# Second attention: keys and eight query heads projected first, the rest between the scores, the bias as a matmul

## The reference, cut to what matters

```
qkv = x @ Wqkv + bqkv            # 256 -> 384 columns: 32 query heads, 8 key heads, 8 value heads, 8 wide each
k, v = repeat(k, 4), repeat(v, 4)
scores = q @ k^T / sqrt(8)       # 512 tokens against 512, two batches, 32 heads
out = softmax(scores) @ v
out @ Wo + bo
```

## Time and profile before

| | |
|---|---|
| median of 3 runs | 675.0 us (671.65 to 675.63) |
| the profiled execution | 669.68 us, span of the trace 667.8 us |
| granted TensorE clock, mean | 0.986 |
| PE busy | 617.4 us, 92% of the span |
| DVE / ACT / POOL busy | 404.4 / 325.1 / 213.2 us |
| start of the attention's projections | 352.73 us from the span's start |
| first score matmul of the loop | 362.19 us |

### The profile page before, as it was taken

One profiled execution on the slowest core, in us unless ns is written; L12 is line 12 of the kernel. 1 busy time (PEld: TensorE's weight loads), 2 busy tenths in 40 slices (PEclk: granted clock), 3 DMA queues, 4 the chain that ended last, 5 costly groups with the idle time before them and its releaser, 6 DMA issues.

```text
span 667.8 us, 11795 instructions
## 1 busy us (share of the span) xinstructions
PE 617.4 (92%) x4298; PEld 408.0 (61%) x4298; DVE 404.4 (61%) x929; ACT 325.1 (49%) x645; POOL 213.2 (32%) x312
## 2 busy tenths in 40 slices
PE   3999999999999988799978999999999999989990
PEld 2887887887888785366665544444444445546660
DVE  4526705632760587533366999989998954743336
ACT  4523423433332224133215589898988875523322
POOL 5870561282073154513333031201010100331331
PEclk9999999999999999899989999999999999999996
DMA  6000200300199992222379994000000000031213
GB/s 220 33 1 33 96 1 20 107 1 1 38 283 299 78 314 77 78 58 81 105 237 346 303 180 3 1 1 2 2 1 2 1 2 1 9 104 55 81 56 126
DMA packets 69000, 57.40 MB, mean 86 GB/s; under 512 B 21520, under 2 KB 64400, under 8 KB 68944
## 3 DMA queue, kind: packets, MB, share of 16 engines
q1 hardware_dynamic: 66736, 50.60, 31.2%
q0 software_dynamic: 2208, 6.05, 2.5%
HBM read 30.78 MB, written 25.85 MB: 85 GB/s over the span
## 4 chain that ended last, share of the span: by engine, by line
PE 73%; DVE 16%; DMA 3%; ACT 3%; issue 2%; POOL 1%; SPq 1%; ACTq 0%; POOLq 0%; DVEq 0%
PE psum L303 9%; PE psum L305 8%; PE psum L304 8%; PE psum L1289 8%; PE psum L1634 8%; DVE mx L1744 7%; PE psum L1606 5%; PE psum L1318 5%; PE psum L1594 5%; PE psum L1619 3%; PE psum L1213 2%; DVE stat L666 2%; PE psum L1564 2%; PE psum L1282 2%; PE psum L1199 1%
## 5 line engine op out<-in xcount | busy, mean ns | idle before, releaser
L1744 DVE TENSOR_REDUCE mx<-psum 128x1 f32<-128x512 f32 x256 | 157.6, 681 | 17.6 <-PE psum L1606 17.5
L1505 ACT ACTIVATE pr<-psum 128x512 f32<-128x512 f32 x256 | 138.0, 598 | 27.9 <-PE psum L1619 26.1
L1634 PE MATMUL psum<-pr,vals 128*32 128x256 f32 x1024 | 77.6, 389 | 0.0
L1619 PE MATMUL psum<-qT,kT 32*128 32x512 f32 x256 | 76.6, 494 | 0.7 <-ACT pr L1505 0.7
L1606 PE MATMUL psum<-kT,qT 32*128 32x512 f32 x256 | 67.7, 488 | 1.7 <-ACT qT L1472 0.7
L1289 PE MATMUL psum<-w_gu,xgT 128*128 x120 | 56.4, 592 | 0.0
L624 POOL DMA_INDIRECT routed_y<-yr,xg x30 | 28.7, 958 | 86.1 <-DVE yr L876 85.5
L1606 PEld LDWEIGHTS psum<-kT,qT 32*128 32x128 f32 x256 | 26.3, 181 | 43.9 <-issue 21.4
L1546 POOL CAST mp<-mx 128x16 bf16<-128x16 f32 x16 | 3.1, 196 | 150.5 <-DVE mx L1744 150.5
L867 DVE SCALAR_TENSOR_TENSOR h<-psum,xg,sg 128x256 f32<-128x256 f32 x30 | 14.5, 484 | 49.8 <-ACT sg L1046 49.8
L1046 ACT ACTIVATE sg<-psum,xg 128x256 f32<-128x256 f32 x30 | 14.2, 474 | 60.4 <-PE psum L1289 60.4
(11 more groups left out here) (214 smaller groups left out, 1406.6 us busy)
## 6 DMA issues: line engine op xcount, KB each, us to landing
sorted_x<-zeros SPq DMA_DIRECT2D x2, 9088.0 KB, 39.2
w_gu<-in_L_ffn_gate_w SPq DMA_DIRECT2D x16, 256.0 KB, 6.2
w_gu<-in_L_ffn_up_w SPq DMA_DIRECT2D x16, 256.0 KB, 6.3
w_d<-in_L_ffn_down_w SPq DMA_DIRECT2D x16, 256.0 KB, 6.6
xg<-sorted_x SPq DMA_DIRECT2D x30, 129.0 KB, 2.2
wk_f<-in_L_attn_Wk SPq DMA_DIRECT2D x4, 512.0 KB, 5.2
wq_f<-in_L_attn_Wq SPq DMA_DIRECT2D x4, 512.0 KB, 6.0
wv_f<-in_L_attn_Wv SPq DMA_DIRECT2D x4, 512.0 KB, 3.7
```

The costliest lines, as they stand in the source:

```text
L1505: nc.scalar.activation(pr[d % 3][:, j], s2_bank(d, j), ACT.Exp, scale=SCALE).then_inc(exp_ready, 1)
L1619: mm(s2_bank(d, j), kT[n // GH][rows, kc * P:(kc + 1) * P], qT2[n % 2][rows, :], start=True, stop=True).then_inc(s2_made, 1)
L1634: last = mm(ps[AV_BANK][j * VW:(j + 1) * VW, cols], vals[:, n // NKV * TB + kc, n % NKV // GH * GH + j, :], pr[d % 3][:, j, cols], start=( ...
L1744: v.tensor_reduce(mx[n % 2][:, t, j:j + 1], s1_bank(c, j), AX.X, ALU.max, negate=True).then_inc(max_read, 1)
```

## The change

- The first four tiles: PE projects only 128 columns at first (the first eight query heads, two groups, and all keys) with `project_first`. ACT rounds the high parts straight from PSUM (`first_hi`), DVE subtracts the low parts of keys and queries straight from PSUM (`first_low`), and this now stands between DVE's statistics of the second half of x. The keys and first queries are turned when the new semaphore `first_stacked` has reached 4.
- The other 256 columns of these tiles (24 query heads and the values) are projected by `project_rest` in two accumulations of 192 and 64 columns: tile 0 ahead of the loop, tiles 1 and 2 in the steps c = 0 and 1, tile 3 at the end of step c = 2. ACT takes each (`take_rest`); POOL rounds and subtracts.
- The bias is a third matmul in each accumulation: a row of ones against the bias row (`with_bias`).
- The second batch's takes (c = 3 to 6) go from DVE to ACT, without the addition. `complete(1)` is cut in three pieces behind the takes of the steps 3, 4 and 5 (2, 3 and 3 tiles).
- The second half of x is turned into banks 6 and 7 in place of 4 and 6, and a turn of queries waits until ACT has copied these.
- Of the ten groups of `keep_warm`, the counts and places change: four and one matmuls ahead of the loop, two in each of the steps 0 and 1.

```diff
-        TURN_X = ((4, 5, 6, 7), (0, 1, 0, 1), (0, 1, 4, 6), (0, 1, 0, 1))
+        TURN_X = ((4, 5, 6, 7), (0, 1, 0, 1), (0, 1, 6, 7), (0, 1, 0, 1))
...
-            close_x(1, 1)
-            l1_y = dve_l1(dve, link, mark, settle, y_tiles, close_stats, sum_x)
+            sum_x(1, 1)
+            l1_y = dve_l1(dve, link, mark, settle, y_tiles, close_stats, sum_x, stats_x)
...
-            def hi_parts(b, t):
-
-                act.wait_ge(qkv_ready, b * TB + t + 1)
-                stack_hi(nc.scalar, b, t, "k").then_inc(k_hi_made[b], 1)
-                stack_hi(nc.scalar, b, t, "q").then_inc(q_hi_made[b], 1)
+            def first_hi(t):
+
+                first = ps[QKV_BANK[t]]
+                act.wait_ge(qkv_made, t + 1)
+                stack_hi(nc.scalar, 0, t, "k", (0, NKV), first[:, FQ:2 * FQ]).then_inc(k_hi_made[0], 1)
+                stack_hi(nc.scalar, 0, t, "q", (0, FH), first[:, 0:FQ]).then_inc(q_hi_made[0], 1)
+
+            def take_rest(t):
+                act.wait_ge(rest_made, t + 1)
+                nc.scalar.activation(qkv[:, t, FQ:FQ + HALF], ps[REST_BANK[t]][:, 0:HALF], ACT.Copy).then_inc(qkv_ready, 1)
+
+            def take(t):
+                act.wait_ge(qkv_made, t + 1)
+                nc.scalar.activation(qkv[:, t, :], ps[QKV_BANK[t]][:, 0:QKV], ACT.Copy).then_inc(qkv_ready, 1)
...
             for what in FIRST:
                 copy_turn(what)
+            take_rest(0)
             normalise(2, 1)
+            take_rest(1)
             for c in range(END):
                 d = c - LAG
+                if c == 1:
+                    take_rest(2)
                 if c == 2:
                     turn_copy(2, 2)
                     turn_copy(2, 3)
-                    complete(1)
+                if c == QKV_AT:
+                    take_rest(3)
+                if QKV_AT <= c < min(QKV_AT + TB, LAG):
+                    take(TB + c - QKV_AT)
+                    if c + 1 < QKV_AT + TB:
+                        complete(1, range(NT)[(c - QKV_AT) * NT // 3:(c + 1 - QKV_AT) * NT // 3])
...
+                if LAG <= c < QKV_AT + TB:
+                    take(TB + c - QKV_AT)
...
+            def with_bias(o, t, cols):
+
+                for c in range(KC):
+                    mm(o, xT[:, c, t * P:(t + 1) * P], cols(wqkv[:, c]), start=(c == 0), stop=False)
+                return mm(o, ones[0:1, :], cols(bqkv[0:1, :]), start=False, stop=True)
+
+            def project_first(t):
+
+                pe.wait_ge(xT_ready, 4 * 2 + t // 2 + 1)
+                with_bias(ps[QKV_BANK[t]][:, 0:2 * FQ], t,
+                          lambda w: w.rearrange("p (a n) -> p a n", a=2)[:, :, 0:FQ]).then_inc(qkv_made, 1)
+
+            def project_rest(t):
+
+                if t >= 2:
+                    pe.wait_ge(qkv_ready, t - 1)
+                with_bias(ps[REST_BANK[t]][:, 0:HALF - FQ], t, lambda w: w[:, FQ:HALF])
+                with_bias(ps[REST_BANK[t]][:, HALF - FQ:HALF], t, lambda w: w[:, KEND:QKV]).then_inc(rest_made, 1)
...
                 elif n >= 2:
                     wait_read(pe, TURNS[n - 1])
+                    pe.wait_ge(xT_ready, 4 * 2 + 4)
                 else:
-                    pe.wait_ge(qkv_ready, TB)
+                    pe.wait_ge(first_stacked, TB)
...
             for t in range(TB):
-                project_qkv(t)
-            pe.wait_ge(qkv_ready, TB)
-            keep_warm(3, 3)
+                project_first(t)
+            keep_warm(4, 3)
             turn(FIRST[0])
-            keep_warm(4, 3)
+            keep_warm(1, 3)
             turn(FIRST[1])
+            project_rest(0)
             for c in range(END):
...
-                if c < QKV_AT:
-                    keep_warm(2, 3)
+                if c < 2:
+                    project_rest(c + 1)
...
-                if c < QKV_AT:
-                    keep_warm(2, 3)
+                if c < 2:
+                    keep_warm(2, AV_BANK)
+                if c == 2:
+                    project_rest(3)
...
+            def first_low(t):
+
+                first = ps[QKV_BANK[t]]
                 dve.wait_ge(k_hi_made[0], t + 1)
-                stack_lo(v, 0, t, "k").then_inc(k_stacked[0], 1)
-
-            for t in range(TB):
-                take(t)
-                if t:
-                    key_lo(t - 1)
-            key_lo(TB - 1)
+                dve.wait_ge(q_hi_made[0], t + 1)
+                stack_lo(v, 0, t, "k", (0, NKV), first[:, FQ:2 * FQ]).then_inc(k_stacked[0], 1)
+                stack_lo(v, 0, t, "q", (0, FH), first[:, 0:FQ]).then_inc(first_stacked, 1)
+
+            stats_x(1, first_low)
...
-                if QKV_AT <= c < QKV_AT + TB:
-                    take(TB + c - QKV_AT)
```

More of the change, by code:

```diff
@@ L77 @@
 SCALE = float(1.0 / HD ** 0.5)
+HALF = NQ * HD
+FH = 2 * GH
+FQ = FH * HD
 def build(nc, a, out):
@@ L212, in build @@
         vals = at("vals", [P, NT, NKV, VW], F32, l1)
-        bqkv, bqkv_in = (at(n, [P, QKV], F32, l1) for n in ("bqkv", "bqkv_in"))
+        bqkv, bqkv_in = (at(n, [P, w], F32, l1) for n, w in (("bqkv", 2 * HALF), ("bqkv_in", QKV)))
         wqkv_in = at("wqkv_in", [P, KC, QKV], F32, l1)
-        wqkv = at("wqkv", [P, KC, QKV], F32, l1)
+        wqkv = at("wqkv", [P, KC, 2 * HALF], F32, l1)
         wo1 = at("wo1", [P, KC, D], F32, l1)
@@ L283, in build @@
         qkv_made, qkv_ready, turn_copied = (sem(n) for n in ("qkv_made", "qkv_ready", "turn_copied"))
+        rest_made, first_stacked, rest_hi = (sem(n) for n in ("rest_made", "first_stacked", "rest_hi"))
         k_hi_made, q_hi_made, k_stacked, q_stacked = (per_layer(n) for n in ("k_hi_made", "q_hi_made", "k_stacked", "q_stacked"))
@@ L700, in sum_x, with stats_x @@
                         mark(ins)
-            def stats_x(half):
+            def stats_x(half, between=None):
                 for i in range(TB):
@@ L706, in stats_x @@
                     tile_stats(x, half * TB + i)
+                    if between:
+                        between(i)
                 close_stats(0, half)
@@ L980, in normalise, with complete @@
                                          scale=rstd[0][:, t:t + 1]).then_inc(xn_ready[half], 1)
-            def complete(p):
-                for t in range(NT):
+            def complete(p, tiles=range(NT)):
+                for t in tiles:
                     if p == BLOCKS - 1:
@@ L1449, in places, with stack_hi @@
             return tile[b][:, t].rearrange("p h (n d) -> p h n d", d=HD)[:, :, first:first + (n - 1) * step + 1:step, :]
[L1451 to L1455, removed]
+        def stack_hi(eng, b, t, kind, heads=None, src=None):
+            tile, n, at_, first = (qs, NQ, Q_AT, 0) if kind == "q" else (ks, NKV, K_AT, HALF)
+            from_, to = heads or (0, n)
+            if src is None:
+                src = qkv[:, b * TB + t, first + from_ * HD:first + to * HD]
+            dst = places(tile, b, t, at_)[:, from_:to].bitcast(F32R)
+            src = heads_of(src).unsqueeze(2).to_broadcast([P, to - from_, 2, HD])
             if eng is nc.scalar:
@@ L1458, in stack_hi, with stack_lo @@
             return eng.tensor_copy(dst, src)
[L1460 to L1465, removed]
+        def stack_lo(eng, b, t, kind, heads=None, src=None):
+            tile, n, first, hi, lo = (qs, NQ, 0, 0, 2) if kind == "q" else (ks, NKV, HALF, 0, 1)
+            from_, to = heads or (0, n)
+            if src is None:
+                src = qkv[:, b * TB + t, first + from_ * HD:first + to * HD]
+            return eng.tensor_tensor(tile[b][:, t, from_:to, lo * HD:(lo + 1) * HD], heads_of(src),
+                                     tile[b][:, t, from_:to, hi * HD:(hi + 1) * HD], ALU.subtract)
         def act_l1(act, normalise, turn_copy, complete):
@@ L1556, in pe_l1 @@
             pe.wait_ge(l1_ordered, L1_ORDERED)
+            def with_bias(o, t, cols):
[11 more added lines that the diff above has]
+                with_bias(ps[REST_BANK[t]][:, HALF - FQ:HALF], t, lambda w: w[:, KEND:QKV]).then_inc(rest_made, 1)
             def project_qkv(t):
                 pe.wait_ge(xT_ready, 4 * 2 + t // 2 + 1)
[L1561 to L1566, removed]
+                pe.wait_ge(qkv_ready, t if t == NT - 1 else TB)
+                with_bias(ps[QKV_BANK[t]][:, 0:QKV], t, lambda w: w[:, 0:QKV]).then_inc(qkv_made, 1)
             def turn(what):
@@ L1583, in turn @@
                 else:
-                    pe.wait_ge(q_stacked[b], TB)
+                    if i * GH < FH:
+                        pe.wait_ge(first_stacked, TB)
+                    else:
+                        pe.wait_ge(q_stacked[b], TB)
                     if kind == "q2":
```

21 lines of the change are left out of this document (10 added, 11 removed).

## The result

The changed kernel takes 687.5 us (683.3 to 691.0) against 673.3 for the kernel before (670.3 to 675.6, four runs each): ratio 1.021, 95% interval 1.017 to 1.026. It is 14 us slower, outside the forecast's range. A run more than 1.5% above the fastest of its kernel is left out of every ratio here: one of E5, one of the kernel before beside E5 to E8 and one beside E9 to E12, and two of E9's four, which therefore has no ratio. The profiled execution of after is its slowest, 691.0 us, span 689.2 us; that of before is one of its fastest.

The account below looks back on a forecast made before the run. PE's chain bounds the steps 2 to 6, so the end of step 6's projection moves all three engines. Terms -2.2 + 3.3 + 2.0 + 1.9 + 0.7 = +5.7 us on 675.0 give 680.7 us, range 674.5 to 685.0.

Parts of the forecast that it names:

- The start: Ahead of the loop: the shorter first projection brings the first score at 360.0 in place of 362.19 us, -2.2 us.
- Rival (d): Start isn't shortened: DVE's subtractions from PSUM and statistics fall behind, first_stacked comes late; +1.2, 681.9 us, chance 0.05.
- rival (c): The bias matmul is dear, by an open second load and dearer switches: +8.4 in all, 683.4 us, chance 0.18.
- the dearer switch: At the bias matmuls: switches of 0.21 us in place of 0.13, 12 of them new on the path, +1.0 us.
- the open second load: At the bias matmuls: the second weight load isn't hidden, 0.107 us more for each of 16, +1.7 us.
- Steps 0 to 5: In the loop on PE's chain: rests and a wait in steps 0 to 2, +3.3 us; bias in steps 3 to 5, +2.0.
- rival (a): Not slower, DVE paces: PE's added work in steps 0 to 6 falls into waiting time; -4.1, 670.9 us, chance 0.12.
- The wait at step 6: PE waits for ACT's copy of q2, now behind a take and three tiles of complete: +1.9 us.
- Rival (b): The wait at step 6 drops the clock to 1.2 GHz for 3.3 us: +1.7, 682.4 us, chance 0.15.
- The sign that the prediction named: Around step 6: granted clock stays at 1.00 from 380 to 390 us.
- The sum: Whole kernel: -2.2 + 3.3 + 2.0 + 1.9 + 0.7 (bias of step 6's projection) = +5.7 us.

Follow-up runs that it names:

- E5: The changed kernel with ACT copying q2 ahead of its take and last tiles of complete, and the bias matmul over all 128 rows: 677.2 us, ratio 1.0076.
- E8: The kernel before with a third matmul of zeros over 128 rows in each of the eight projections: 675.5 us, ratio 1.0043.
- E9: The start's part of the change alone, second batch as in the kernel before: 673.5, 671.5, 684.8 and 684.6 us, no ratio.
- E12: E11 with the two warming matmuls in each of the steps 0 and 1 kept: 669.8 us, ratio 0.9976.
- E1: The changed kernel with ACT's order turned: copy of q2 first, then take of tile 6, last three tiles of complete later: 678.0 us against 671.9, ratio 1.0105.
- E6: The kernel before with complete cut in three pieces, so that the copy of q2 waits; no bias matmul: 678.4 us against 673.1, ratio 1.0110.
- E10: The kernel before with the second batch's part alone: one-row bias for tiles 4 to 7, ACT's takes, complete in three pieces: 678.7 us, ratio 1.0111.
- E13: E9 with the bias matmul over 128 rows in place of one: 12 runs from 670.2 to 676.3 us, ratio 1.0011.
- E7: The kernel before with a third matmul of zeros over one row in each of the eight projections: 680.2 us, ratio 1.0112.
- E11: E13 with values ahead of keys in the weights, each rest one accumulation of 256 columns, no warming in steps 0 and 1: 669.2 us against 671.7, ratio 0.9967.

## Why the prediction was wrong

- **The start, -2.2 us: mis-sized, and in after's trace wrong in sign.** At full clock it is -0.9 (E1), since a one-row bias costs a switch on both sides and the prediction counted one: 1.05 us for a tile, not 0.77. In after's trace another 4.4 us come from the clock: 12.97 us from the first projection to the first score against 8.6. Rival (d) fell: E1's chain from the first projection to the first score is PE's alone. Of rival (c) the dearer switch is there, the open second load isn't: two bias instructions over 128 columns take 0.41 us with their switch.
- **Steps 0 to 5, +5.3: right to 0.1 us**, and so is what it rests on, that PE paces and the takes which leave DVE buy nothing; rival (a) fell.
- **The wait at step 6, +1.9: right**, 2.11 us of idle time ended by ACT's copy, with take and `complete` in front of it.
- **Rival (b), the step that failed.** "The wait drops the clock" got a chance of 0.15 and a price of 1.7 us: "half of 3.3 us is lost". Its own sum puts the clock at nothing. It happened, and it was 13.7 us of low clock, not 3.3. The price came from the earlier trace rows, where PE recovered while it did nothing but warming matmuls at full height without a gap. Behind step 6 PE does scores over 32 rows, and waits for ACT and DVE; after's low stretch there, E6's and E10's were 13.7, 17 and 17 us. From the end of step 5's projection to DVE's 48th maximum, the last of step 11, the trace of before has 394.63 - 378.02 = 16.6 us, after 411.39 - 387.08 = 24.3: +7.7, of which 1.9 is the wait and 0.8 the bias, so 5.0 are left for the clock. E6 shows the same with the wait alone: some 6 us. The sign that the prediction named, a clock of 1.00 from 380 to 390, was met all the same: the fall came at 390.5, just behind it. The rows of before, then of after:

```profile
378.02 0.42 PE psum L1606
...
394.63 1.29 DVE mx L1744 x2
```

```profile
387.08 0.02 issue
...
411.39 1.29 DVE mx L1797 x2
```

- **What the prediction didn't have at all** is the low clock over the start. The prediction took the clock there as given by before's trace. The idle 2.24 us ahead of it are no edit of the change: in before the warming matmuls ran into a low stretch and lasted longer, which left 0.57 us of idle time; in after they were done early. In before:

```profile
348.67 1.38 PE L1128 MATMUL psum<-ident 128*128 128x128 f32 x10 [0.57 <-DVE nmean L676]
```

  E1's trace has before's pattern with the changed kernel's start, so this varies from run to run. Whether the change also made the start more sensitive to it, by one-row matmuls, is suggested by the times of E9 and E13 and not shown by a trace; that pieces of 128 columns do was not tested.
- **The sum** at full clock would be -0.9 + 5.3 + 1.9 + 0.8 = +7.1 where the prediction has +5.7. The other half of the 14 us, by subtraction, is clock: 5 us behind the wait, and in some runs 4.4 over the start or 4.4 at the end of the loop, which the prediction didn't have either.

What stays open: E1, E5, E7, E8, E11 and E13 have a low stretch of 3.4 or 6.8 us near step 7 with no idle group over 0.6 us, and several runs of the kernel before (mean clock 0.978 against 0.986 in its profiled run) may have one, as far as the mean clock tells. PE's last wait ahead of the stretch, for ACT's exponentials in step 7, is 0.5 to 0.6 us in all six, and it is 0.51 us in the traces of before and E9 too, where the clock stays at 1.00. No run shows what brings it, nor what brings the stretch at the end of the loop. So a wait isn't the only thing that lowers the clock there; what E6 shows is that the wait alone makes the low stretch long, 17 us.

## What to carry to other kernels

Price a new PE wait not by its length but by the work that follows: if that is sparse (few rows, waits of its own), 1.5 us of idle time can cost 5 us more. A bias as a matmul should fill all rows, since one row costs two switches. Compare traces at several fixed points before a gain is put down to an edit: E1 got its number back partly from stretches that it didn't touch. When an engine's work is moved, look at what then stands in front of a copy that PE waits for.

## What the runs showed of the hardware

- A wait of 1.54 us on PE was followed by 17 us at 1.2 GHz (E6); one of 1.56 us in the earlier trace rows by none. The same wait as that of the earlier trace rows, 1.5 to 1.6 us for a transfer, was followed by 3.4 us at 1.2 GHz in the traces of E9, E12 and E13 (1.61, 1.54 and 1.64 us), and by none in those of after, E1, E10 and E11 (1.51 to 1.59). So the length of one idle time doesn't tell whether the clock falls. The Trainium skill (TensorE: Matmul & The Clock Gate, "Why this matters for your kernels") warns of idle gaps between bursts of matmuls; the gaps it names are longer than the 1.54 us of E6.
- A bias matmul of one row and 384 columns costs 0.84 us and makes the next tile's projection 0.2 us longer than one over 128 rows (0.65 us) does (E7, E8).
- A matmul over 64 columns with weights of 128 columns takes hardly less than one over 128 columns: four in 0.39 us, 0.098 each (E5), against the 0.107 that the prediction took.
